# Adding two recurrences' sums by accumulating DMAs instead of on VectorE, in an attention and feed-forward kernel

## The chip, the cores and the metric

The kernel runs on one NeuronCore of a Trainium2 chip. The metric is the device time of one execution in microseconds (us); lower is better.

## The reference, cut to what matters

Four sequences (B = 4) of 256 tokens with 256 channels pass through one layer: a gate, causal attention with 16 heads, a second gate, and a feed-forward part with ternary weights.

```python
def _bi_wkv(r, k, v, w, u, time_emb):            # both gates; k and v are the same side input
    tf = sigmoid(sum(time_emb, axis=-1))[:, None, None]
    decay = exp(-exp(w))[None, :] * (0.5 + 0.5 * tf[:, :, 0])
    ek = exp(minimum(k, 30.0)); ekv = ek * v
    # nf, df: a = a * decay + ekv_t, b = b * decay + ek_t over the tokens; nb, db: the same in reverse
    euk = exp(minimum(u[None, None, :] + k, 30.0))
    num = nf + nb - ekv + euk * v
    den = df + db - ek + euk
    return sigmoid(r) * (num / maximum(den, 1e-08)) * (0.8 + 0.2 * tf)
x = x + attention(_bi_wkv(x, side, side, w1, u1, cond))
h = _bi_wkv(x, side, side, w2, u2, cond)
x = x + (silu(h @ ternary(W_up).T) * (h @ ternary(W_gate).T)) @ ternary(W_down).T
```

## The kernel before, in words

Channels lie on the 128 partitions, in two tiles (`ct`) of 256 tokens, so one sequence of one quantity is 128x512 in f32. Everything is in SBUF after the first loads. Each engine has its own program, written out by hand, and the engines are ordered by semaphores alone.

**A gate.** For gate `c` (0 the first, 1 the second) and sequence `b`, `ek[b % 3]` holds the products (half 0) and the exponentials (half 1). Four forward scans (`forward`, L599, two per half, 128x256 each) write `fwd[c]`, and four backward scans (`backward`, L611) write `bwd[c]`. `extra[c]` holds exp(u + k), made on ScalarE, and its product with k, made on GpSimd (`extra_products`, L245). `add_extra` adds `extra[c]` into `fwd[c]` and `sums` adds `bwd[c]` into it, each one instruction of 128x1024. `bound_denominator` (L628) bounds the denominator, ScalarE takes its reciprocal as a logarithm and an exponential (`first_reciprocal`, L358 and L360), `refine` does two products on VectorE, and `first_wkv` or `second_wkv` gives the gate's output. For sequences 0 and 1 the first gate is done in one piece by `first_gate`.

**Attention.** The gate's output goes through the projections of keys and queries (L980) and of values (L990). ScalarE and VectorE split keys and queries into f16 halves (`high_halves`, `low_halves`), six DMAs of SP stack them (`stack<-halves`), and PE makes scores in six groups (`scores`). VectorE takes row maxima (`maxima`), PE turns them, SP stores them in the stack, PE makes transposed scores (`score_t`), ScalarE exponentiates (`exp_probs`), and PE weighs the values (`weigh`). After the last `weigh` come the row reciprocals on ScalarE (L406, L408), `normalize` on VectorE (L690), `project` on PE (L1207) and `residual` on VectorE (L696).

**Feed-forward.** With f = b - 1, iteration `b` does the feed-forward part of sequence f beside the attention scores of sequence b. `ffn_input` multiplies 1 + tanh with the second gate's output (L705) into `x2`; ScalarE rounds it to `x2_hi` in f16 (`high_input`, L437), and `low_input` (L710) gives `x2_lo`. `up_gate(f, e)` for the eight tiles `e` of hidden channels (L1015) takes both halves; ScalarE does the silu (L445), VectorE the product (`gate`, L753). Two tiles are a group `g`: ScalarE rounds it (`high_hidden`, L452), GpSimd subtracts (`low_hidden`, L270), and `down(f, g)` (L1043) multiplies by the down weights; the last group is split on VectorE (`last_halves`). `finish` writes the result.

**Order.** VectorE alternates `maxima(b, j)` and `gate(f, j)` for j from 0 to 5, then does gates 6 and 7 with other work of the gates between them. In this text, turn b to b + 1 is the stretch from the last `weigh` of b to the third group of scores of b + 1. The last sequence has a tail in two halves of tokens.

Of the kernel before, what the change touches and what calls it, by code (L numbers as in the profile page):

```python
# [44 lines left out]
def build(nc, x_d, k_d, cond_d, vec_d, wqkv_d, wo_d, wup_d, wgate_d, wdown_d, out_d):  # L45
    with ExitStack() as ctx:
# [78 lines left out]
        w_in = [sem(f"w_in{i}") for i in range(3)]  # L125
        k_top_done, roundneg_made = sem("k_top_done"), sem("roundneg_made")
# [108 lines left out]
        def _(pool):  # L235
# [12 lines left out]
            def add_extra(c, b):  # L248
# [38 lines left out]
            values_of_keys(0)  # L287
            extra_products(0, 0)
# [16 lines left out]
            extra_products(0, 1)  # L305
            bound_keys()
            pool.wait_ge(vec_in, 16)
            bound_sums(1)
            bound_sums(0)
            values_of_keys(2)  # L310
            for b in range(1, B):
                more = b + 1 < B
                if more:
                    if b == 1:
                        pool.wait_ge(x2lo_done, b)
                    pool.wait_ge(fwd_done[0], 4 * b + 8)
# [8 lines left out]
                low_hidden(b - 1, 1)  # L325
                low_hidden(b - 1, 2)

        @block.scalar
        def _(act):
# [13 lines left out]
            def extra_exp(c, b):  # L343
                if b:
                    act.wait_ge(fwd_extra[c], b)
# [145 lines left out]
            def ternary_weights(i):  # L491
# [3 lines left out]
                nc.scalar.activation(w_tern[i][:, :], w_raw[i][:, :], ACT.Sign,  # L495
                                     bias=round_neg[:, 0:1]).then_inc(tern_done, 1)

            for b in range(B):
                more, f = b + 1 < B, b - 1
                if b:  # L500
# [6 lines left out]
                    high_input(f)  # L507
# [4 lines left out]
                    if b == 1:  # L512
                        ternary_weights(2)
# [861 lines left out]
```

## Time and profile before

| | |
|---|---|
| time, median of 3 runs | 180.51 us (178.92 to 180.75) |
| the profiled execution's own time | 180.7 us |
| its span, first to last instruction | 178.9 us |
| outside the span | 1.8 us |
| mean granted TensorE clock | 0.985 of full |
| busy: PE, VectorE (DVE), ScalarE (ACT), GpSimd (POOL) | 147.7, 154.7, 116.5, 53.2 us |

The rows further down come from that one execution. In a timeline a row is: start us, duration us, engine, line, operation, tiles, shapes, count, and in brackets how long the engine had been idle before it and what ended that. Matmuls overlap in the pipeline, so their rows' durations overlap too, and the distance from start to start is the better measure.

### The profile page before, as it was taken

The page shows a single profiled execution, that of the slowest core. Times are in us where ns is not written, and L with a number is a line of the kernel's source. Part 1 is how long each engine was busy: PE and PEld are TensorE (multiplying, and loading weights), DVE is VectorE, ACT ScalarE, POOL GpSimd, SP SyncE. Part 2 cuts the span into 40 slices and gives each one's busy share as a digit, 9 for nine tenths or more (in the row PEclk, how much of TensorE's full clock was granted, in tenths as well). Part 3 has the DMA queues.
Part 4 walks back from the last instruction along what each step waited for, and adds up shares of the span by engine and source line. Part 5 has one row for each costly group of instructions (what it writes and reads, how often), then busy time and mean ns, then how long its engine had stood idle before and what let it go on. Part 6 is the DMA issues. An engine that isn't in the chain of part 4 may idle for free. (4 is left out here: it accounts for less than half of the span.)

```text
span 178.9 us, 3837 instructions
## 1 busy us (share of the span) xinstructions
PE 147.7 (83%) x1550; PEld 98.8 (55%) x1550; DVE 154.7 (86%) x259; ACT 116.5 (65%) x187; POOL 53.2 (30%) x51
## 2 busy tenths in 40 slices
PE   0007897968949998999998899999989999997991
PEld 0007882233337854774676457745855576686870
DVE  0599998999998778999999999999697999986672
ACT  2547986989645795479557734885574458875640
POOL 8920052999600049440000194400002223000000
PEclk9999999999996999999999999999999999999997
DMA  4999322000000310000033000000420000010001
GB/s 107 359 430 421 121 75 103 4 2 0 5 0 0 119 60 0 0 5 0 0 132 108 0 4 0 2 4 0 148 92 0 2 5 0 4 62 2 4 0 59
DMA packets 5706, 10.91 MB, mean 61 GB/s; under 512 B 760, under 2 KB 4024, under 8 KB 5304
## 3 DMA queue, kind: packets, MB, share of 16 engines
q1 hardware_dynamic: 5400, 10.52, 15.5%
q8 instruction: 12, 0.20, 0.5%
q10 hardware_dynamic: 288, 0.14, 0.4%
q14 instruction: 6, 0.05, 0.1%
HBM read 6.43 MB, written 1.05 MB: 42 GB/s over the span
## 5 line engine op out<-in xcount | busy, mean ns | idle before, releaser
L245 POOL TENSOR_TENSOR extra<-extra,k_t 128x512 f32<-128x512 f32 x8 | 10.3, 1293 | 79.3 <-DVE fwd L599 40.2
L686 DVE TENSOR_REDUCE row_max<-wide 128x4 f32<-128x1024 f32 (+1 forms) x24 | 28.8, 1217 | 1.0 <-PE wide L1070 1.0
L401 ACT ACTIVATE probs<-wide 128x1024 f32<-128x1024 f32 x24 | 23.8, 1018 | 1.1 <-PE wide L1095 0.7
L445 ACT ACTIVATE silu<-attn_ps,up_scale 128x256 f32<-128x256 f32 x24 | 11.2, 472 | 19.5 <-PE attn_ps L1015 17.6
L611 DVE TENSOR_TENSOR_SCAN bwd<-ek,decay 128x255 f32<-128x255 f32 x32 | 21.2, 707 | 0.0
L599 DVE TENSOR_TENSOR_SCAN fwd<-decay,ek 128x256 f32<-128x256 f32 x32 | 21.1, 706 | 0.0
L1215 PE MATMUL wide<-ones 128*128 128x128 f32 x24 | 5.4, 425 | 14.5 <-DVE fwd L804 14.5
L270 POOL TENSOR_TENSOR hid_lo<-hid,hid_hi 128x512 f16<-128x512 f32 x9 | 12.4, 1379 | 15.1 <-ACT hid_hi L452 15.1
L1117 PE MATMUL attn_ps<-probs,v_pad 128*32 128x256 f32 (+1 forms) x192 | 12.6, 334 | 3.6 <-ACT probs L401 3.6
L1015 PE MATMUL attn_ps<-x_hi,w_tern 128*128 128x256 f16 x96 | 14.2, 274 | 1.3 <-ACT x_hi L437 0.8
L1015 PE MATMUL attn_ps<-x_lo,w_tern 128*128 128x256 f16 x96 | 13.9, 273 | 0.0
L1065 PE MATMUL wide<-mask_qk,identity_b 128*128 128x256 bf16 (+1 forms) x48 | 11.0, 311 | 2.9 <-DMA stack<-halves 1.8
L1215 PEld LDWEIGHTS wide<-ones 128*128 128x128 f32 x24 | 5.2, 331 | 14.5 <-issue 14.5
L1117 PE MATMUL attn_ps<-probs,ones_pad 128*32 128x256 f32 (+1 forms) x192 | 12.4, 331 | 0.0
L753 DVE TENSOR_TENSOR hid<-silu,attn_ps 128x256 f32<-128x256 f32 x24 | 9.9, 411 | 2.8 <-ACT silu L445 2.7
L1015 PEld LDWEIGHTS attn_ps<-x_hi,w_tern 128*128 128x128 f16 x96 | 8.3, 98 | 5.1 <-issue 2.2
L263 POOL TENSOR_SCALAR uk_top<-k_t,vec 128x768 f32<-128x768 f32 (+1 forms) x4 | 11.0, 2738 | 0.4
L1043 PE MATMUL acc_ps<-hid_hi,w_tern 128*128 128x256 f16 x64 | 9.8, 273 | 0.5 <-DVE hid_hi L769 0.5
L1015 PEld LDWEIGHTS attn_ps<-x_lo,w_tern 128*128 128x128 f16 x96 | 9.2, 98 | 1.3 <-DVE x_lo L710 0.2
L358 ACT ACTIVATE rec<-fwd 128x512 f32<-128x512 f32 x8 | 5.0, 631 | 7.4 <-DVE fwd L628 4.0
L980 PE MATMUL turn_ps<-wkv,wqkv 128*128 128x256 f32 x32 | 9.4, 445 | 0.5 <-DVE wkv L657 0.5
L1043 PE MATMUL acc_ps<-hid_lo,w_tern 128*128 128x256 f16 x64 | 9.7, 273 | 0.0
(147 smaller groups left out, 346.4 us busy)
## 6 DMA issues: line engine op xcount, KB each, us to landing
stack<-halves SPq DMA_DIRECT2D x24, 128.0 KB, 2.1
w_raw<-wup_d SPq DMA_DIRECT2D x1, 1024.0 KB, 11.3
w_raw<-wgate_d SPq DMA_DIRECT2D x1, 1024.0 KB, 13.0
w_raw<-wdown_d SPq DMA_DIRECT2D x1, 1024.0 KB, 14.9
out_d<-x_t SPq DMA_DIRECT2D x4, 256.0 KB, 2.3
wqkv<-wqkv_d SPq DMA_DIRECT2D x1, 768.0 KB, 7.0
k_t<-k_d SPq DMA_DIRECT2D x1, 768.0 KB, 8.4
x_t<-x_d SPq DMA_DIRECT2D x1, 768.0 KB, 9.8
```

What stands on the lines that cost most here:

```text
L263: nc.gpsimd.tensor_scalar(uk_top[c][:, :, ct * T:(ct + 1) * T], k_t[:, 2 - c:B, ct, :], vec[:, u:u + 1], CLAMP, ALU.add, ALU.min).then_inc ...
L270: nc.gpsimd.tensor_tensor(hid_lo[:, g % 2], hid[:, g % 2], hid_hi[:, g % 2], ALU.subtract).then_inc(hidlo_done, 1)
L401: nc.scalar.activation(probs[:, j, :], flat(wide[j % 2][:, :, :]), ACT.Exp, scale=SOFTMAX_SCALE).then_inc(prob_done, 1)
L445: nc.scalar.activation(silu[:, e % 2], up, ACT.Silu, scale=up_scale[:, 0:1]).then_inc(silu_done, 1)
L599: nc.vector.tensor_tensor_scan(fwd[c][:, half, ct * T:(ct + 1) * T], d, ek[b % 3][:, half, ct * T:(ct + 1) * T], 0.0, ALU.mult, ALU.add).t ...
L611: nc.vector.tensor_tensor_scan(bwd[c][:, half, at], ek[b % 3][:, half, after], d, 0.0, ALU.add, ALU.mult).then_inc(bwd_done[c], 1)
L686: nc.vector.tensor_reduce(out, src, AX.X, ALU.max).then_inc(max_done, 1)
L1015: mm = nc.tensor.matmul(attn_ps[:, e % 2, w * T:(w + 1) * T], w_tern[w][:, at:at + P], half[:, dt, :], start=(w == 0 and dt == 0 and x == ...
L1043: mm = nc.tensor.matmul(acc_ps[:, dt, :], w_tern[2][:, at:at + P], half[:, g % 2, e, :], start=first, stop=(g == NG - 1 and e == EG - 1 an ...
L1065: nc.tensor.matmul(tile[:, a, :, width - P:width], identity_b[:, :], mask_qk[:, :].unsqueeze(1).broadcast_to([P, per, P]), start=True, sto ...
L1117: mm = nc.tensor.matmul(attn_ps[lo:lo + 32, what, ct * T + q0:(ct + 1) * T], left, prob[:, i % 2, i // 2, :], start=(j == 0), stop=(second ...
L1215: nc.tensor.matmul(wide[0][:, 0, 0:P], ones[:, :], ones[:, :], start=True, stop=True)
```

## The change

- **Sums by DMA.** `send_extra` and `send_backward` are DMAs issued by GpSimd that add one tile of 128x1024 f32 (512 KB) into `fwd[c]` in SBUF. They take the place of `add_extra` and `sums` for the first gate of sequences 2 and 3 and the second gate of sequences 0, 1 and 2, ten DMAs in all. On VectorE eight instructions of 128x1024 go, on GpSimd two. The second gate of sequence 3 stays on VectorE. A pair of DMAs is a chain: the second waits until the first has landed, and GpSimd waits with it.
- **Scans moved.** The second gate's forward scans stand between gates 5, 6 and 7, where the first gate's last backward scans and `sums(0, b + 1)` stood (sequence 3: the second gate's backward scans). The first gate's scans of the next sequence follow `finish`, the low halves and `second_wkv`. For sequence 3 the second gate's backward scans stand at the turn.
- **Reciprocals.** `refine(1, b)` stands at the end of iteration b, ahead of `normalize`.
- **Feed-forward input.** `x2_hi` is written by VectorE (two instructions of 128x256), then `x2` by one of 128x512; `high_input` on ScalarE is gone. No scans stand any more between `ffn_input` and `maxima(b, 0)`.
- **Group 2.** `down(f, 2)` does both halves ahead of the first transposed scores, where its low half followed two groups of them.
- **Start and weights.** The first two products of sequence 0 go from GpSimd to VectorE. The down weights' last step on ScalarE is done in two pieces, after silu 1 and silu 3, where it stood whole ahead of silu 0. `bound_sums(0)` comes ahead of `bound_sums(1)` on GpSimd.

```diff
+            def send_extra(c, b):
                 pool.wait_ge(prod_done[c], b + 1)
                 pool.wait_ge(fwd_done[c], 4 * b + 4)
-                nc.gpsimd.tensor_tensor(fwd[c][:, :, :], fwd[c][:, :, :], extra[c][:, :, :],
-                                        ALU.add).then_inc(fwd_extra[c], 1)
+                pool.dma_start(fwd[c][:, :, :], extra[c][:, :, :], accum_op=ALU.add).then_inc(extra_in[c], 16)
+
+            def send_backward(c, b):
+                wait_extra_added(pool, c, b)
+                pool.wait_ge(bwd_done[c], 4 * b + 4)
+                pool.dma_start(fwd[c][:, :, :], bwd[c][:, :, :], accum_op=ALU.add).then_inc(sum_in[c], 16)
...
-            values_of_keys(0)
-            extra_products(0, 0)
...
             def extra_exp(c, b):
                 if b:
-                    act.wait_ge(fwd_extra[c], b)
+                    wait_extra_added(act, c, b - 1)
...
                     for e in range(ET):
                         silu_up(f, e)
                         if e % EG == 0 and e:
                             high_hidden(f, e // EG - 1)
+                        if b == 1 and e in (1, 3):
+
+                            ternary_weights(2, slice(1024 * (e // 2), 1024 * (e // 2 + 1)))
...
                     dve.wait_ge(tanh1_done, 2 * b + ct + 1)
-                    nc.vector.scalar_tensor_tensor(x2[:, part], x2[:, part], 1.0, wkv2[:, b, part],
-                                                   ALU.add, ALU.mult).then_inc(x2_done, 1)
-
-            def low_input(b):
+                    nc.vector.scalar_tensor_tensor(x2_hi[:, ct, :], x2[:, part], 1.0, wkv2[:, b, part],
+                                                   ALU.add, ALU.mult).then_inc(x2hi_done, 1)
                 dve.wait_ge(x2hi_done, 2 * b + 2)
+                nc.vector.scalar_tensor_tensor(x2[:, :], x2[:, :], 1.0, wkv2[:, b, :],
+                                               ALU.add, ALU.mult).then_inc(x2_done, 1)
+                dve.wait_ge(x2_done, b + 1)
...
                     up_gate(f, 7)
-                    down(f, 2, 0)
+                    down(f, 2)
```

VectorE in iteration 2, from gate 5 to the last group's halves, before:

```order
L753 TENSOR_TENSOR hid<-silu,attn_ps 128x256
L611 SCALAR_TENSOR_TENSOR bwd0<-ek0,decay 128x255 x2
L753 TENSOR_TENSOR hid<-silu,attn_ps 128x256
L623 TENSOR_TENSOR fwd0<-fwd0,bwd0 128x1024
L753 TENSOR_TENSOR hid<-silu,attn_ps 128x256
L760 CAST hid_hi<-hid 128x512
```

And after:

```order
L771 TENSOR_TENSOR hid<-silu,attn_ps 128x256
L616 SCALAR_TENSOR_TENSOR fwd1<-decay,ek2 128x256 x2
L771 TENSOR_TENSOR hid<-silu,attn_ps 128x256
L616 SCALAR_TENSOR_TENSOR fwd1<-decay,ek2 128x256 x2
L771 TENSOR_TENSOR hid<-silu,attn_ps 128x256
L778 CAST hid_hi<-hid 128x512
```

Four forward scans of the second gate stand there now in place of two backward scans and a sum of the first.

VectorE at the turn from sequence 2 to 3, from `first_wkv` on, before:

```order
L657 SCALAR_TENSOR_TENSOR wkv1<-fwd0,gain,err0 128x512
L599 SCALAR_TENSOR_TENSOR fwd1<-decay,ek2 128x256 x4
L784 SCALAR_TENSOR_TENSOR x_t<-acc_ps,out_scale,x_t 128x512
L617 TENSOR_TENSOR fwd1<-fwd1,extra1 128x1024
L623 TENSOR_TENSOR fwd1<-fwd1,bwd1 128x1024
L628 TENSOR_SCALAR fwd1<-fwd1 128x512
L671 SCALAR_TENSOR_TENSOR halves<-turn_ps,vec,halves 128x256 x2
L671 SCALAR_TENSOR_TENSOR halves<-acc_ps,vec,halves 128x256 x2
L690 TENSOR_TENSOR heads_t<-attn_ps,row_rec 128x512
L638 TENSOR_TENSOR err1<-fwd1,rec1 128x512
```

And after:

```order
L674 SCALAR_TENSOR_TENSOR wkv1<-fwd0,gain,err0 128x512
L802 SCALAR_TENSOR_TENSOR x_t<-acc_ps,out_scale,x_t 128x512
L645 TENSOR_SCALAR fwd1<-fwd1 128x512
L688 SCALAR_TENSOR_TENSOR halves<-turn_ps,vec,halves 128x256 x2
L628 SCALAR_TENSOR_TENSOR bwd1<-ek0,decay 128x255 x2
L688 SCALAR_TENSOR_TENSOR halves<-acc_ps,vec,halves 128x256 x2
L655 TENSOR_TENSOR err1<-fwd1,rec1 128x512
L660 SCALAR_TENSOR_TENSOR err1<-err1,rec1 128x512
L707 TENSOR_TENSOR heads_t<-attn_ps,row_rec 128x512
L679 SCALAR_TENSOR_TENSOR wkv2<-fwd1,gain,err1 128x512
L628 SCALAR_TENSOR_TENSOR bwd1<-ek0,decay 128x255 x2
```

The denominator (L628 before, L645 after) now stands behind `finish` and waits for the second DMA of its pair; two backward scans of sequence 3 stand ahead of the low halves of the queries. At the turn from 1 to 2 the first gate's four forward scans stand behind `finish` as well.

GpSimd in iteration 1, with the semaphores it waits for, after (before, the first DMA was an addition on GpSimd and the three others were not there):

```order
L263 TENSOR_TENSOR extra0<-extra0,k_t 128x512 [waits ex_exp0,x2lo_done]
L269 DMA fwd0<-extra0 128x1024 [waits fwd_done0,prod_done0]
L263 TENSOR_TENSOR extra1<-extra1,k_t 128x512 [waits ex_exp1]
L292 TENSOR_TENSOR hid_lo<-hid,hid_hi 128x512 [waits hidhi_done]
L257 TENSOR_TENSOR ek0<-ek0,k_t 128x512 [waits ek_exp]
L292 TENSOR_TENSOR hid_lo<-hid,hid_hi 128x512 [waits hidhi_done]
L274 DMA fwd0<-bwd0 128x1024 [waits bwd_done0,extra_in0]
L292 TENSOR_TENSOR hid_lo<-hid,hid_hi 128x512 [waits down_done,hidhi_done]
L269 DMA fwd1<-extra1 128x1024 [waits fwd_done1,prod_done1]
L274 DMA fwd1<-bwd1 128x1024 [waits bwd_done1,extra_in1]
```

The pair of the second gate follows the last `low_hidden`, and the next instruction of GpSimd waits for the next iteration.

## Rows read from the trace of the kernel before

**Rows 1.** Windows: us, busy time and count by engine, granted clock, DMA share

```profile
51.00:53.20 2.20, 0.01 (x2) 0.01 (x2) 2.13 (x4) 1.54 (x2) 0.00 (x0) 1.00 0.00 0
54.40:57.60 3.20, 3.20 (x12) 2.64 (x9) 3.00 (x6) 1.34 (x3) 0.00 (x0) 0.54 0.00 0
79.00:93.60 14.60, 14.60 (x196) 8.65 (x194) 14.32 (x24) 10.79 (x16) 0.43 (x1) 1.00 0.11 37
93.60:103.30 9.70, 7.98 (x57) 4.92 (x54) 9.34 (x18) 7.47 (x15) 1.13 (x1) 1.00 0.16 55
```

**Rows 2.** Timeline of PE, iterations 0 to 3

```profile
54.39 3.44 PE L980 MATMUL turn_ps<-wkv,wqkv 128*128 128x256 f32 x8
...
77.90 0.60 PE L1043 MATMUL acc_ps<-hid_hi,w_tern 128*128 128x256 f16 x4
...
91.74 0.42 PE L1117 MATMUL attn_ps<-probs,v_pad 128*32 128x128 f32 x8
...
93.62 1.99 PE L990 MATMUL wide<-wqkv,wkv 128*128 128x256 f32 x8
...
104.79 0.38 PE L1065 MATMUL wide<-mask_qk,identity_b 128*128 128x256 bf16 x2
...
129.17 1.99 PE L990 MATMUL wide<-wqkv,wkv 128*128 128x256 f32 x8
...
139.41 0.39 PE L1065 MATMUL wide<-mask_qk,identity_b 128*128 128x256 bf16 x2
```

**Rows 3.** Timeline of ACT: three places where it waits or sets the turn

```profile
51.59 0.63 ACT L348 ACTIVATE extra<-uk_top 128x512 f32<-128x512 f32 x1 [2.57 <-DVE fwd L617]
...
94.39 0.63 ACT L408 ACTIVATE row_rec<-row_rec 128x512 f32<-128x512 f32 x1
...
127.33 0.63 ACT L358 ACTIVATE rec<-fwd 128x512 f32<-128x512 f32 x1 [1.83 <-DVE fwd L628]
```

**Rows 4.** Groups of VectorE by line

```profile
L623 DVE TENSOR_TENSOR fwd<-fwd,bwd 128x1024 f32<-128x1024 f32 x6 | 7.3, 1222 | 0.1
...
L617 DVE TENSOR_TENSOR fwd<-fwd,extra 128x1024 f32<-128x1024 f32 x4 | 4.9, 1217 | 0.1
...
L628 DVE TENSOR_SCALAR fwd<-fwd 128x512 f32<-128x512 f32 x6 | 2.5, 424 | 0.1
```

**Rows 5.** Timeline of VectorE

```profile
6.55 1.27 DVE L584 TENSOR_SCALAR extra<-extra 128x512 f32<-128x512 f32 x1 [0.35 <-ACT extra L352]
...
8.42 0.77 DVE L816 TENSOR_SCALAR exp_t<-exp_t 128x4 f32<-128x4 f32 x1 [0.27 <-ACT exp_t L465]
...
50.35 1.21 DVE L617 TENSOR_TENSOR fwd<-fwd,extra 128x1024 f32<-128x1024 f32 x1
...
67.59 0.42 DVE L753 TENSOR_TENSOR hid<-silu,attn_ps 128x256 f32<-128x256 f32 x1 [1.03 <-ACT silu L445]
...
98.50 0.87 DVE L696 SCALAR_TENSOR_TENSOR x_t<-attn_ps,bo_v,x_t 128x256 f32<-128x256 f32 x2
99.54 0.76 DVE L705 SCALAR_TENSOR_TENSOR x<-x,wkv 128x256 f32<-128x256 f32 x2 [0.17 <-ACT x L431]
...
121.37 2.43 DVE L599 TENSOR_TENSOR_SCAN fwd<-decay,ek 128x256 f32<-128x256 f32 x4
...
147.41 2.18 DVE L611 TENSOR_TENSOR_SCAN bwd<-ek,decay 128x255 f32<-128x255 f32 x2
```

**Rows 6.** Timeline of GpSimd

```profile
6.28 1.26 POOL L239 TENSOR_TENSOR ek<-ek,k_t 128x512 f32<-128x512 f32 x1
...
77.42 2.01 POOL L270 TENSOR_TENSOR hid_lo<-hid,hid_hi 128x512 f16<-128x512 f32 x1 [2.73 <-ACT hid_hi L452]
...
147.63 1.41 POOL L270 TENSOR_TENSOR hid_lo<-hid,hid_hi 128x512 f16<-128x512 f32 x1 [2.73 <-ACT hid_hi L452]
```

**Rows 7.** DMA issues: KB each, us from issue to landing

```profile
stack<-halves SPq DMA_DIRECT2D x24, 128.0 KB, 2.1
w_raw<-wup_d SPq DMA_DIRECT2D x1, 1024.0 KB, 11.3
```

More of the change, by code:

```diff
@@ L125, in build @@
         w_in = [sem(f"w_in{i}") for i in range(3)]
+        extra_in, sum_in = ([sem(f"{n}{c}") for c in range(2)] for n in ("extra_in", "sum_in"))
         k_top_done, roundneg_made = sem("k_top_done"), sem("roundneg_made")
@@ L325, in _ @@
                 low_hidden(b - 1, 1)
+                if more:
+                    send_backward(0, b + 1)
                 low_hidden(b - 1, 2)
+                if more:
+                    send_extra(1, b)
+                    send_backward(1, b)
         @block.scalar
@@ L811, in _ @@
             clamp_keys(0)
+            dve.wait_ge(ek_done, 1)
+            nc.vector.tensor_tensor(ek[0][:, 0, :], ek[0][:, 1, :], flat(k_t[:, 0]), ALU.mult).then_inc(ekv_done, 1)
             clamp_extra(0, 0)
@@ L814, in _ @@
             nc.vector.tensor_reduce(tsum[:, :], cond_b[:, :, :], AX.X, ALU.add).then_inc(tsum_done, 1)
+            dve.wait_ge(ex_done[0], 1)
+            nc.vector.tensor_tensor(extra[0][:, 0, :], extra[0][:, 1, :], flat(k_t[:, 0]),
+                                    ALU.mult).then_inc(prod_done[0], 1)
             dve.wait_ge(expt_done, 1)
@@ L853, in _ @@
                         normalize(f)
+                        second_wkv(f)
                         if more:
-                            backward(0, b + 1, 1, (1,))
-                        refine(1, f)
-                        second_wkv(f)
+                            backward(0, b + 1, 0)
+                        else:
+                            backward(1, b, 0)
                     residual(f)
                     ffn_input(f)
-                    if more:
-                        forward(0, b + 1, 0, (0,))
-                    low_input(f)
-                    if more:
-                        forward(0, b + 1, 0, (1,))
                     maxima(b, 0)
@@ L937, in _ @@
                     dve.wait_ge(bo_done, 1)
-                    forward(0, 2, 1)
-                    backward(0, 2, 1)
+                    for half in (1, 0):
+                        forward(0, 2, half)
+                    for half in (1, 0):
+                        backward(0, 2, half)
                     first_product(1, 0)
@@ L1020, in up_gate, with down @@
                     mm.then_inc(ug_done, 1)
-            def down(b, g, halves=2):
+            def down(b, g):
                 parts = ((hid_hi, hidhi_done), (hid_lo, hidlo_done))
@@ L1029, in down @@
                         pe.wait_ge(y_done, b)
-                if b == 0 and g == 0:
-                    pe.wait_ge(tern_done, 3)
-                for half, done in parts if halves == 2 else parts[halves:halves + 1]:
+                if b == 0 and g % 2 == 0:
+                    pe.wait_ge(tern_done, 3 + g // 2)
+                for half, done in parts:
                     if g == NG - 1:
@@ L1046, in down @@
                                                   skip_group_check=True)
-                if halves:
-                    mm.then_inc(down_done, 1)
+                mm.then_inc(down_done, 1)
             def rows(b, side, a, pair, n, lo, hi):
@@ L1288, in _ @@
                     tail_score_t(1)
-                    down(f, 2, 1)
                     down(f, 3)
@@ L1300, in _ @@
                 score_t(b, 1)
-                down(f, 2, 1)
                 down(f, 3)
```

98 lines of the change are left out of this document (45 added, 53 removed).

## The prediction

> **What bounds the kernel now.** I read the windows first. Between 79.0 and 93.6 PE is busy for 14.60 of 14.60 us, and VectorE for 14.32 [rows 1]. Both are full, but PE alone has no idle time at all, so work that leaves VectorE there doesn't shorten the stretch. In the next window, the turn from sequence 1 to 2 (93.6 to 103.3), PE is busy 7.98 of 9.70 us. Next I read PE's timeline for where it is held. In iteration 0 it idles from 51.0 to 53.2 and then runs 3.2 us at a granted clock of 0.54, which is the lower of its two levels, 1.2 GHz [rows 1]; the key projection at 54.39 has a row of 3.44 us there, where eight matmuls of the same shape have 1.99 at 93.62 [rows 2]. Last I read what ScalarE waits for: 2.57 us on VectorE's addition L617 ahead of 51.59, and 1.83 us on L628 ahead of 127.33 [rows 3]. So the sums on VectorE cost time in two kinds of places: in iteration 0 and at the turns. In between, PE's own work decides.
>
> I take the change in five terms: start, iteration 0, group 2's low half, turns, tail. They are differences against the span of 178.9 us.
>
> **Start: -0.5.** The two products leave GpSimd. VectorE pays two instructions of about 0.67 us for it (1222 ns for 1024 columns is 0.61 for 512, plus start-up [rows 4]). But its own small steps there are drawn out today: the bounding at 6.55 takes 1.27 us beside GpSimd's product at 6.28, and exp_t, four columns, 0.77 [rows 5, 6]. The same kind of bounding takes 0.42 elsewhere (L628 [rows 4]), and four columns about 0.15. So VectorE wins 0.85 + 0.62 and fills idle time of 0.35 + 0.27 [rows 5] against 1.34 paid: 0.7 at best. ScalarE's step between tsum and exp_t keeps some of it. I take 0.5; the bounds are 0 and 0.7. All of iteration 0 hangs on this chain, so it moves everything.
>
> **Iteration 0: -2.7.** ScalarE's `extra_exp(1, 1)` now waits for a DMA issued some 15 us earlier, so the wait of 2.57 goes, the last exponential comes 3 us earlier, and PE starts the key projection when `wkv1` is there, near 51.0 where it was 54.39 [rows 2, 3]. That isn't the gain yet, since VectorE comes late next. Its list from 50.35 to gate 0 at 67.59 takes 17.24 us [rows 5]. The new list: the bounding 0.35; eight scans at 2.43 for four [rows 5], 4.85, where there were L617, L623 (2.44, [rows 4]) and four scans, so no gain yet; three products 1.8; low keys, `wkv2`, low queries 2.4; residual and the wait for tanh 1.1. That is 10.5, at 60.85. Then `x2_hi` 0.7, at 61.55, when PE can begin. PE's way from there: first halves 0.9, two groups of scores 1.75, low half of tile 0 0.45, silu 0.5 on ScalarE, so gate 0 at 65.15 at the latest; VectorE comes by 64.7 with its own list (x2 0.6, x2_lo 0.65, a maximum 1.15). The row of 67.59 shows 1.03 us of waiting for silu, behind the down weights' last step on ScalarE, which now stands behind silu 1. Gate 0 at 64.7 to 65.15 is 2.4 to 2.9 earlier. A new risk lies in it: PE is done with the query projection near 54.7 and waits for `normalize` until about 56.7, 2.0 us, nearly the 2.2 us after which its clock fell to 0.54 before [rows 1]. If it falls again, `project`, eight such matmuls, takes 1.5 more and the residual comes 0.5 later. I take -2.7 of -2.2 to -2.9.
>
> **Group 2's low half: +1.5.** `down(f, 2)` low now stands ahead of the transposed scores, in PE's full stretch. PE is done with the high half at 78.33 (77.90 and 0.44 for four matmuls [rows 2]). GpSimd's `hid_lo` starts at 77.42 and took 2.01 beside VectorE's sum, and 1.41 beside scans in iteration 3, where VectorE's two scans took 2.18 in place of 1.26 [rows 5, 6]. Now scans stand beside it in each iteration. With 1.41 it is there at 78.83, so PE idles 0.5, three times: +1.5. The bounds are 0.3 (1.16, uncontended) and 1.1 (2.01) each, so +0.8 to +3.3. VectorE's gate 7 comes 0.8 later for the drawn-out scans. That is hidden: PE does two groups of transposed scores (1.3 us) ahead of `down(f, 3)`, and the first gate's output, 0.55 later, still meets PE's key projection, which is 0.5 later itself.
>
> **Turns: -1.65.** I count on PE from `values` to the fourth group of scores: 93.62 to 104.79 is 11.17, 129.17 to 139.41 is 10.24 [rows 2]. The new chain from `values`: row reciprocals 1.3 (L406 and the row at 94.39 [rows 3]), `normalize` 0.65, project 1.85, so the residual starts at +3.95 where it was +4.88 (98.50 [rows 5]). From the residual to x2's first instruction 1.04 (98.50 to 99.54 [rows 5]), where `x2_hi` stands now, 0.7; x2 0.6; x2_lo 0.67. The low half is there at +7.0, PE's scores and high half are done by then, and low half 0.9 and the wait for a maximum (1.15 after x2_lo) bring the third group of scores to +8.35 and the fourth to +9.88, by the step of 1.53 between groups. That is 1.3 less at the turn 1 to 2 and 0.36 less at 2 to 3. The stack DMA has its source earlier too: the reciprocal ahead of the high queries no longer waits 1.83 [rows 3]. What carries this is VectorE's room: L617 and L623 (2.44) leave each turn and L623 the gates, 3.66 an iteration [rows 4], against some 0.7 for `x2_hi`. The first gate's scans that filled it (0.6 each) now lie in the shadow of `project` and of the query projection.
>
> **Tail: -0.2.** Sequence 3's denominator comes 2.4 us earlier (four scans [rows 5]), but ScalarE takes it only behind its fifth exponential, nearly as before, and PE's weighing behind it keeps its length. I take -0.2, bounds 0 and -0.5.
>
> **What the DMAs may cost: 0.** Nothing in the trace adds by DMA or is issued by GpSimd, so I bound one DMA (issue to landing, D). `stack<-halves` moves 128 KB in 2.1 us [rows 7]. The accumulation reads two tiles of 512 KB. The low end is that row, 2.1. In the loading phase 1024 KB landed in 11.3 us behind other loads, a slow row [rows 7]; that is 5.6 for 512 KB, and with 2 us for GpSimd's preparation, as long as it was at most over 512 columns (2.01 [rows 6]), the high end is 7.6. Neither row is near, the one small and the other crowded, so I take the middle, 4.8; the queues are nearly empty at these places (DMA share 0.11 to 0.16 [rows 1]). How much is free? The second gate's forward scans end at about 79.35 in the frame of the old trace. The denominator may be as late as 90.7: the query projection ends at 91.74 [rows 2], shifted by 0.5, the high halves take 0.8, and ahead of the low queries stand 0.35 + 0.8 + 1.2 of VectorE's work. 11.35 us for two DMAs: free up to D = 5.65, then 2 us for each us of D, at two turns, so 4(D - 5.65). For the first gate one DMA issued at about 74.7 must land by 80.9, D up to 6.2.
>
> The Trainium skill (DMA: Bandwidth & Descriptors, Anatomy of one DMA, SWDGE path) gives about 2.0 us + bytes / 436e3 for such a DMA, 3.2 us here without the addition; by that the DMAs stay hidden with over 2 us to spare, which no row here shows. The Trainium skill (SBUF — State Buffer, Who interferes with whom) states a rule against this change: descriptor generation on GpSimd is starved while VectorE is in a two-port mode, as its boundings of 0.42 us would be; that would add at most 0.4 to a D, and the sum stays as it is unless D is above 5.2 already.
>
> **Sum.** -0.5 - 2.7 + 1.5 - 1.65 - 0.2 = -3.55. The profiled execution took 180.7, so 177.15; the median of the runs is 0.2 lower, 180.51, so I say **177.0**. With the inner bounds of the terms the sum lies between -2.0 and -5.0, so 175.5 to 178.5.
>
> **Rivals.**
> - **The DMAs are slow (ends slower than before).** The mechanism: VectorE waits in `bound_denominator(1, b)` for the pair, with both low halves, the backward scans and `normalize` behind it, and scores wait for the stack. The place: both turns. The gain is used up at 4(D - 5.65) = 3.55, D = 6.5. At D = 7.5 it costs 7.4: 184.4. Between 5.9 and 7.1 the result is within 1%. For it: two reads and a write, unknown unit. Against: empty queues. 0.12 for within 1%, 0.14 for slower by more.
> - **GpSimd's low half is late.** It takes 2.0 as at 77.42 [rows 6], PE loses 1.1 three times: +3.3 in place of 1.5, and the clock falls once more in iteration 0: 179.1, within 1%. For it: that duration is what two of three iterations show today. Against: it stood beside `tensor_tensor`, which scans replace. 0.12.
> - **More than forecast.** `hid_lo` uncontended, the full start and iteration 0, tail -0.5: below 175.8. 0.10.
>
> **How the numbers follow.** The forecast has 0.52. A measurement of this kernel can tell about 1% from no change, so faster is below 178.7 and slower above 182.3. Faster: 0.52 + 0.10 = 0.62; same 0.12 + 0.12 = 0.24; slower 0.14. For 8 in 10 the range leaves out 0.07 below, and the upper part of the slow DMAs: 175.4 to 181.8.
>
> **What would show it.** (1) First scan near 9.7 where it was 10.2. (2) ScalarE without the wait at 51.6, the key projection at full clock near 50.5. (3) Gate 0 of iteration 1 at 64.2 to 64.7, the start included. (4) PE idle 0.3 to 1.1 ahead of `down(f, 2)` low. (5) D below 5.65, and no wait of VectorE in L645 that passes on to the low queries. (6) No wait of PE for the stack at the turns. The forecast is wrong if L645 waits over 2 us at a turn, or if PE's idle time between 79 and 93 grows by more than 1 us.

## The result, and the profile after

The kernel after takes **177.89 us** (median of 6 runs, 177.87 to 177.95), the kernel before 180.47 beside it (6 runs, 178.92 to 181.73): ratio 0.990, 95% interval 0.9858 to 0.9942. All ratios here leave out runs over 1.5% above a kernel's fastest. The profiled execution took 177.95, its span is 176.2 where it was 178.9. The forecast was 177.0, within 175.4 to 181.8: the direction came true, the gain is 2.6 us where 3.5 was said.

One thing has to be known first. The kernel before has no single time. Its 74 runs beside all kernels of this study lie in three bands: 38 at 178.30 to 179.02 (median 178.86), 31 at 179.94 to 180.77 (median 180.49), 5 at 181.3 to 181.9. The profiled execution, 180.7, belongs to the second. The six runs of the kernel after lie in one band, 0.08 us wide. Against the first band it gains 1.0 us, against the second 2.6.

The timeline of PE of the kernel after, at the rows that answer to [rows 2]:

```profile
37.71 2.29 PE L1009 MATMUL attn_ps<-mask_kq,identity_b 128*128 128x512 bf16 x5
...
51.43 1.99 PE L992 MATMUL turn_ps<-wkv,wqkv 128*128 128x256 f32 x8
...
55.84 1.99 PE L1218 MATMUL attn_ps<-heads_t,wo 128*128 128x256 f32 x8 [0.70 <-DVE heads_t L707]
...
75.44 0.61 PE L1055 MATMUL acc_ps<-hid_lo,w_tern 128*128 128x256 f16 x4 [0.39 <-POOL hid_lo L292]
75.89 0.38 PE L1101 MATMUL wide<-mask_kq,identity_b 128*128 128x256 bf16 x2
...
90.71 1.99 PE L1002 MATMUL wide<-wqkv,wkv 128*128 128x256 f32 x8
...
98.24 1.05 PE L1027 MATMUL attn_ps<-x_lo,w_tern 128*128 128x256 f16 x8 [0.62 <-DVE x_lo L728]
99.37 0.39 PE L1076 MATMUL wide<-mask_qk,identity_b 128*128 128x256 bf16 x2
...
101.00 0.39 PE L1076 MATMUL wide<-mask_qk,identity_b 128*128 128x256 bf16 x2
...
125.96 1.99 PE L1002 MATMUL wide<-wqkv,wkv 128*128 128x256 f32 x8
```

The key projection has 1.99 us at full clock instead of 3.44. Group 2's low half waits 0.39 us for GpSimd (0.40 at 110.69 and 0.39 at 145.93). `values` of sequence 2 comes at 90.71 where it was 93.62, and the fourth group of scores at 101.00 where it was 104.79. The windows of the kernel after over the places of [rows 1] (us, busy time and count of PE, PEld, DVE, ACT, POOL, granted clock, DMA share, GB/s):

```profile
51.00:53.20 2.20, 2.20 (x28) 1.82 (x19) 2.20 (x5) 1.77 (x3) 0.00 (x0) 1.00 0.00 0
...
76.00:90.70 14.70, 14.70 (x197) 8.57 (x194) 12.95 (x25) 10.78 (x16) 1.73 (x2) 1.00 0.50 118
90.70:101.00 10.30, 9.40 (x70) 5.88 (x67) 9.57 (x16) 6.57 (x12) 2.44 (x3) 1.00 0.12 41
```

PE has no idle time left from 51.0 to 53.2, stays full in the stretch of the transposed scores, and in the turn idles 0.90 us instead of 1.72. (The last window runs on to the fourth group of scores; before, it is 1.72 us to that point too, in the window 93.6 to 104.8.) ScalarE's timeline where [rows 3] has the wait of 2.57 us:

```profile
48.39 0.62 ACT L371 ACTIVATE extra<-uk_top 128x512 f32<-128x512 f32 x1
49.34 1.03 ACT L424 ACTIVATE probs<-wide 128x1024 f32<-128x1024 f32 x1 [0.32 <-PE wide L1106]
```

It is gone. VectorE's timeline at the start, at gate 0 and at the turn, its bounding at the second turn, then GpSimd's, then the DMA issues (KB each, us to landing), which answer to [rows 5 to 7]:

```profile
6.99 0.51 DVE L601 TENSOR_SCALAR extra<-extra 128x512 f32<-128x512 f32 x1
...
9.36 1.27 DVE L616 TENSOR_TENSOR_SCAN fwd<-decay,ek 128x256 f32<-128x256 f32 x2
...
64.14 0.42 DVE L771 TENSOR_TENSOR hid<-silu,attn_ps 128x256 f32<-128x256 f32 x1 [0.62 <-ACT silu L462]
...
86.61 0.43 DVE L645 TENSOR_SCALAR fwd<-fwd 128x512 f32<-128x512 f32 x1 [0.73 <-DMA fwd<-bwd]
86.96 0.87 DVE L688 SCALAR_TENSOR_TENSOR halves<-turn_ps,vec,halves 128x256 f16<-128x256 f32 x2
87.74 1.26 DVE L628 TENSOR_TENSOR_SCAN bwd<-ek,decay 128x255 f32<-128x255 f32 x2
89.81 0.88 DVE L688 SCALAR_TENSOR_TENSOR halves<-acc_ps,vec,halves 128x256 f16<-128x256 f32 x2 [0.81 <-ACT halves L404]
```

```profile
121.42 0.43 DVE L645 TENSOR_SCALAR fwd<-fwd 128x512 f32<-128x512 f32 x1 [2.64 <-DMA fwd<-bwd]
```

```profile
73.99 1.40 POOL L292 TENSOR_TENSOR hid_lo<-hid,hid_hi 128x512 f16<-128x512 f32 x1 [1.93 <-ACT hid_hi L469]
76.49 0.87 POOL L269 DMA_DIRECT2D fwd<-extra  x1 [1.10 <-DVE fwd L616]
82.16 0.85 POOL L274 DMA_DIRECT2D fwd<-bwd  x1 [4.80 <-ACT extra L371]
```

```profile
fwd<-extra POOLq DMA_DIRECT2D x5, 512.0 KB, 5.2
fwd<-bwd POOLq DMA_DIRECT2D x5, 512.0 KB, 4.5
```

The pair is issued at 76.49 and 82.16. VectorE waits 0.73 us for it in L645, but then again 0.81 us for ScalarE's high queries ahead of the low ones, so nothing of the first wait is passed on. At the second turn it waits 2.64 us in L645, since the four scans of 2.43 us that stand ahead of it at the first turn aren't there, and then 1.25 us for the high queries. These wait 0.71 us for TensorE in their turn, so that wait isn't passed on either.

### The profile page after: what moved, and what is told of

It is laid out like the page before. It is cut to its first block, busy times and chain, and to the rows that moved or that the text cites. A ratio compares the mean times of both kernels' runs of the same rounds, so it can differ in the third digit from the quotient of the medians.

```text
span 176.2 us, 3834 instructions
## 1 busy us (share of the span) xinstructions
PE 147.7 (84%) x1550; PEld 97.2 (55%) x1550; DVE 148.5 (84%) x256; ACT 115.1 (65%) x182; POOL 54.4 (31%) x57
## 4 chain that ended last, share of the span: by engine, by line
PE 37%; DVE 22%; issue 6%; ACT 4%; POOL 2%; POOLq 1%; DVEq 0%; ACTq 0%
PE attn_ps L1128 7%; DVE row_max L703 7%; PE acc_ps L1055 4%; PE attn_ps L1027 4%; PE wide L1206 3%; PE wide L1101 2%; DVE hid L771 2%; PE attn_ps L1218 2%; PE wide L1106 2%; PE acc_ps L992 2%; PE turn_ps L992 2%; POOL hid_lo L292 2%; PE attn_ps L1170 2%; DVE bwd L628 1%; PE turn_ps L1183 1%
## 5 line engine op out<-in xcount | busy, mean ns | idle before, releaser
L263 POOL TENSOR_TENSOR extra<-extra,k_t 128x512 f32<-128x512 f32 x7 | 9.7, 1382 | 62.6 <-DVE x_lo L728 43.8
L616 DVE TENSOR_TENSOR_SCAN fwd<-decay,ek 128x256 f32<-128x256 f32 x32 | 23.1, 770 | 0.0
L628 DVE TENSOR_TENSOR_SCAN bwd<-ek,decay 128x255 f32<-128x255 f32 x32 | 20.0, 677 | 0.0
L1226 PE MATMUL wide<-ones 128*128 128x128 f32 x24 | 4.5, 369 | 13.7 <-DVE fwd L822 13.7
L292 POOL TENSOR_TENSOR hid_lo<-hid,hid_hi 128x512 f16<-128x512 f32 x9 | 11.1, 1238 | 15.4 <-ACT hid_hi L469 15.4
L1226 PEld LDWEIGHTS wide<-ones 128*128 128x128 f32 x24 | 4.3, 282 | 13.7 <-issue 13.7
L285 POOL TENSOR_SCALAR uk_top<-k_t,vec 128x512 f32<-128x512 f32 (+1 forms) x4 | 11.1, 2769 | 0.4
L1081 PE MATMUL wide<-stack 63*128 63x128 f16 (+1 forms) x128 | 9.4, 246 | 0.0
L1101 PE MATMUL wide<-mask_kq,identity_b 128*128 128x256 bf16 (+1 forms) x36 | 8.5, 319 | 0.0
```

Of the source, the lines that this page charges most:

```text
L285: nc.gpsimd.tensor_scalar(uk_top[c][:, :, ct * T:(ct + 1) * T], k_t[:, 2 - c:B, ct, :], vec[:, u:u + 1], CLAMP, ALU.add, ALU.min).then_inc ...
L292: nc.gpsimd.tensor_tensor(hid_lo[:, g % 2], hid[:, g % 2], hid_hi[:, g % 2], ALU.subtract).then_inc(hidlo_done, 1)
L616: nc.vector.tensor_tensor_scan(fwd[c][:, half, ct * T:(ct + 1) * T], d, ek[b % 3][:, half, ct * T:(ct + 1) * T], 0.0, ALU.mult, ALU.add).t ...
L628: nc.vector.tensor_tensor_scan(bwd[c][:, half, at], ek[b % 3][:, half, after], d, 0.0, ALU.add, ALU.mult).then_inc(bwd_done[c], 1)
L1101: nc.tensor.matmul(tile[:, a, :, 0:P], identity_b[:, :], mask_kq[:, :].unsqueeze(1).broadcast_to([P, per, P]), start=True, stop=False, ski ...
```

## Experiments

### The bands of the kernel before: is it the clock?

In the profiled execution of before, TensorE waits 2.60 us for the last `probs` of iteration 0, and then runs at 0.54 of its clock [rows 1, 2]:

```profile
53.19 0.43 PE L1117 MATMUL attn_ps<-probs,v_pad 128*32 128x128 f32 x8 [2.60 <-ACT probs L401]
```

The experiment fills that wait:

```diff
                             weigh(0, j - 1)
+                    pe.wait_ge(neg_done, 1)
+                    keep_busy(8, flat(turn_ps[:, :, :]))
                     weigh(0, NT - 1)
```

> Changed: the kernel before, with eight filler matmuls (bf16, 512 columns, into a bank that is overwritten later) ahead of the last weighing of iteration 0, where TensorE waits 2.60 us for ScalarE's last exponential. Nothing is left out. The runs of the kernel before lie at 178.3 to 179.0 us (16 of 34 in the last two comparisons), near 180.5 (most of the others) and at 181.3 to 181.9; its profiled run shows the clock at 0.54 for some 3 us behind that wait. Theory: the levels are whether the clock falls there, and the fall costs 1.6 us. With TensorE busy through the wait the clock stays, and all runs lie at 178.9, within 0.3 us. Then 1.6 of the 2.6 us that the change gained are the clock's, and only 1.0 the work's. Rival: the levels have another cause (transfers, the start), and the spread from 178.3 to 181.9 stays.

Measured: 178.88 us, 12 runs: 9 at 178.45 to 179.03, 3 at 179.52 to 179.56, further off than the 0.3 us expected; nothing near 180.5 or above, where 12 of the 23 runs of before beside it lie (180.17 to 181.85). The ratio to before is 0.9977 (0.9946 to 1.0008). PE's timeline of this run and its windows:

```profile
51.04 1.90 PE L997 MATMUL turn_ps<-mask_kq,identity_b 128*128 128x512 bf16 x8
53.22 0.43 PE L1117 MATMUL attn_ps<-probs,v_pad 128*32 128x128 f32 x8 [0.28 <-ACT probs L401]
...
54.23 1.99 PE L980 MATMUL turn_ps<-wkv,wqkv 128*128 128x256 f32 x8
```

```profile
54.23:57.60 3.37, 3.37 (x20) 2.98 (x17) 3.37 (x7) 2.37 (x5) 0.00 (x0) 1.00 0.00 0
```

The last weighing starts at the same time as before (53.22, it was 53.19), so the work waits as long; only the clock is kept. Gate 0 then stands at 65.98 instead of 67.59 [rows 5]: **1.61 us** of the profiled execution are the clock's. This is the distance between the two lower bands. Why three runs took 179.5 isn't shown: none of them was profiled. Their mean granted clock is the lowest of the twelve, 0.980 and 0.981 beside 0.984 to 1.000, which speaks for a smaller fall elsewhere.

Two limits. First, no run of before in its lowest band was profiled. That the clock stays at this place in those runs follows from this experiment alone. Their mean granted clock doesn't tell: 0.977 to 0.990 in the lowest band, 0.981 to 0.990 in the second (only the highest band stands out, with 0.968). Second, a fall can cost nothing. In the profiled executions of this kernel and of the kernel after, the granted clock is 0.57 on average over 4 us (38 to 42 and 37 to 41), which it isn't in that of before. In after, five matmuls at 37.71 take 2.29 us there, in before 1.24. Yet this kernel's last weighing comes at 53.22 as said, and of the kernel after one run with a mean clock of 0.981 and one with 1.000 took 177.89 and 177.88. What counts is where the clock falls.

### The start alone

The kernel before, with `values_of_keys(0)` and `extra_products(0, 0)` off GpSimd and on VectorE:

```diff
-            values_of_keys(0)
-            extra_products(0, 0)
...
+            nc.vector.tensor_tensor(ek[0][:, 0, :], ek[0][:, 1, :], flat(k_t[:, 0]), ALU.mult).then_inc(ekv_done, 1)
...
+            nc.vector.tensor_tensor(extra[0][:, 0, :], extra[0][:, 1, :], flat(k_t[:, 0]),
+                                    ALU.mult).then_inc(prod_done[0], 1)
```

> Changed: the kernel before, with the start of the kernel after alone: the two extra products of sequence 0's first gate on VectorE. Nothing is left out. Theory: the start is a term of its own, worth the 0.84 us by which the first scan moved in the kernel after: 180.47 - 0.8 = 179.7 us. Rival: in the kernel before iteration 0 waits for something else (values, a later load), which takes some of it back: 180.2 or more.

Measured: bands again, 7 of 12 runs at 177.88 to 177.90, 4 at 179.50 to 179.55, one at 180.84; ratio to before 0.9929 (0.9886 to 0.9972). The lowest band is 0.97 under that of before, and **as low as the whole change** (177.89). The forecast of 179.7 was worked out from a median that mixes bands; band by band its 0.8 comes near. The profiled run is one of the second band; its windows show where the clock went, behind the same wait of 2.60 us:

```profile
50.00:52.30 2.30, 0.08 (x4) 0.08 (x8) 2.23 (x4) 1.54 (x2) 0.00 (x0) 1.00 0.00 0
52.30:53.90 1.60, 1.60 (x32) 1.26 (x32) 1.60 (x4) 1.26 (x2) 0.00 (x0) 0.54 0.00 0
53.90:57.00 3.10, 3.10 (x14) 2.56 (x11) 2.63 (x5) 1.33 (x3) 0.00 (x0) 0.69 0.00 0
```

So in the lowest band the start is worth all of the change's 1.0 us, and everything else in it comes out at about nothing.

### Group 2's low half back where it was

```diff
-                    down(f, 2)
+                    down(f, 2, 0)
...
                 score_t(b, 1)
+                down(f, 2, 1)
                 down(f, 3)
```

> Changed: the kernel after, with the low half of group 2 put back behind the first two groups of transposed scores, where the kernel before has it. Nothing is left out. Theory: the low half's new place costs 0.54 to 0.58 us in each of three iterations (PE waits 0.39 to 0.40 us for GpSimd's low half, and VectorE's scans beside it are drawn out). Moved back, the low half is awaited by nobody: 177.89 - 1.5 to 1.7 = 176.2 to 176.4 us. Rival: the 0.4 us are only taken from another wait, of the transposed scores for VectorE's or ScalarE's work behind it, and the time stays at 177.9. A second rival: the low half comes later for group 3, whose hidden tiles take the same buffer, and PE waits there: over 178.2.

Measured: 178.09 us (178.05 to 178.11), 0.992 of before (0.9888 to 0.9952): 0.2 **slower** than after. The first rival came true, and the trace names the wait that takes over, in iterations 1 and 2 (iteration 2 has the same row at 111.39, with 0.74):

```profile
71.20 0.88 POOL L274 DMA_DIRECT2D fwd<-bwd  x1
72.44 0.55 SPq L243 DMA_DIRECT2D stack<-neg_max  x1
75.80 0.39 PE L1102 MATMUL wide<-mask_kq,identity_b 128*128 128x256 bf16 x2 [0.73 <-DMA stack<-neg_max]
```

This is the transfer of the maxima, 8 KB, issued by SP at 72.44; the transposed scores need it. In the kernel before it was issued at 75.88, the scores began at 78.33, 2.45 us later, and TensorE didn't wait. In this run it takes 3.36 us from the issue to the scores. In iteration 3 the scores start without a wait and this kernel gains about 0.57 on after. The difference between the iterations: in 1 and 2 GpSimd has just issued `fwd<-bwd` of the first gate (71.20), 512 KB; in iteration 3 there is no such DMA.

Two kernels test that. The first has the low half behind in iteration 3 alone (`down(f, 2, 2 if more else 0)`), the second keeps it behind everywhere and takes the first gate's DMAs away instead:

```diff
-            return b >= 2 if c == 0 else b < B - 1
+            return c == 1 and b < B - 1
...
-                    send_extra(0, b + 1)
+                    add_extra(0, b + 1)
...
+                    sums(0, b + 1)
                     bound_denominator(0, b + 1)
```

> Changed: the kernel after, with group 2's low half behind the first two groups of transposed scores in iteration 3 alone; in iterations 1 and 2 it stands as in the kernel after. Nothing is left out. Theory: the earlier place pays where an accumulating DMA of the first gate is in the way of the small transfer of the maxima (TensorE waited 0.73 and 0.74 us for it in iterations 1 and 2 when the low half stood behind, and not at all in iteration 3, which has no such DMA). So iteration 3 alone gains what the low half costs there, 0.57 us: 177.3 to 177.4. Rival: the wait for the maxima isn't tied to the DMA, and iteration 3 gains nothing: 177.9.

> Changed: the kernel after with group 2's low half behind the first two groups of transposed scores in all iterations, and with the first gate's two sums of sequences 2 and 3 as instructions (the addition on GpSimd, the sum on VectorE ahead of its bounding); the second gate keeps its DMAs. Nothing is left out. Theory: with no accumulating DMA under way when the maxima are sent, TensorE's waits of 0.73 and 0.74 us for their transfer go. VectorE's 1.22 us come back ahead of the key projection, where some 0.35 us are free, so 0.9 is lost: 178.09 - 1.47 + 1.7 = 178.3, between 177.5 and 178.6. Rival: the maxima's transfer is late for a cause of its own (its queue, its start 0.2 us nearer to the scores) and the waits stay: 179.5 or more.

Measured: 177.36 us (177.35 to 177.48; ratio 0.989, 0.9845 to 0.9934), as the theory said; and 179.33 (179.31 to 179.53; 0.9987, 0.9956 to 1.0017). The second is 1.0 slower than forecast and near its rival's time, yet its rows decide between the two. The window 72.4 to 76.0 (columns as in the windows above), first with the low half back and the DMA in the air, then without the DMA, and the issue of the maxima and the scores of the latter:

```profile
72.40:76.00 3.60, 2.87 (x27) 2.26 (x24) 3.60 (x6) 2.33 (x5) 1.40 (x1) 1.00 0.74 148
```

```profile
72.40:76.00 3.60, 3.60 (x34) 2.71 (x32) 3.60 (x6) 2.33 (x5) 1.41 (x1) 1.00 0.01 2
```

```profile
72.61 0.55 SPq L243 DMA_DIRECT2D stack<-neg_max  x1
...
75.06 0.38 PE L1107 MATMUL wide<-mask_kq,identity_b 128*128 128x256 bf16 x2
...
84.37 1.99 PE L997 MATMUL turn_ps<-wkv,wqkv 128*128 128x256 f32 x8 [0.94 <-DVE wkv L678]
```

With a DMA share of 0.01 the maxima, issued at 72.61, are there by 75.06, in 2.45 us or less, and PE doesn't wait. The cost is on the other side: VectorE's 1.22 us come back, and the key projection waits 0.94 for `wkv1`. Another 0.44 goes because TensorE, which comes 0.74 earlier, now meets VectorE's halves of group 3 unfinished (its matmuls at 76.94 and 77.67 don't follow at once). That is 1.38 lost for 0.74 gained, at each of two places, where 0.9 was expected. The Trainium skill (Trainium Kernel Development and Optimization, Key Constraints) says that DMAs from all issuing queues run on the same 16 engines and interleave; a small transfer of SP beside a large one of GpSimd is that, and the trace agrees: 3.36 against at most 2.45 us.

### How much room has the pair?

```diff
+                if c == 1 and b:
+                    pool.wait_ge(tern_done, 1)
+                    pool.dma_start(w_raw[0][:, 0:1024].rearrange("p (a q) -> p a q", a=2), extra[1][:, :, :]).then_inc(copy_in, 16)
+                    pool.wait_ge(copy_in, 16 * b)
                 pool.dma_start(fwd[c][:, :, :], extra[c][:, :, :], accum_op=ALU.add).then_inc(extra_in[c], 16)
```

> Changed: the kernel after, with one more DMA of 512 KB on GpSimd's queue (a plain copy of extra[1] into a tile that is free by then), awaited ahead of the accumulating pair of the second gate in iterations 1 and 2. Nothing is left out. Theory: the pair has little room, about 0.8 us at the first turn and 1.25 at the second (by those much the high queries on ScalarE end what the low queries on VectorE wait for). A copy that takes 4 us to land then passes on 3.2 + 2.75 us: about 183.8, between 182 and 185.5 for a copy of 3.2 to 4.8 us. Rival: the pair has room beyond what these waits show, since the rows behind it shift together: below 180.

Measured: 184.77 us (184.59 to 184.85), 1.030 of before (1.0252 to 1.0342). GpSimd's and VectorE's timelines at the first turn:

```profile
76.46 0.61 POOL L272 DMA_DIRECT2D w_raw<-extra  x1 [1.11 <-issue]
80.72 0.87 POOL L274 DMA_DIRECT2D fwd<-extra  x1 [3.65 <-DMA w_raw<-extra]
85.48 0.86 POOL L279 DMA_DIRECT2D fwd<-bwd  x1 [3.88 <-DMA fwd<-extra]
```

```profile
91.77 0.43 DVE L650 TENSOR_SCALAR fwd<-fwd 128x512 f32<-128x512 f32 x1 [5.92 <-DMA fwd<-bwd]
```

The bounding comes 5.16 later than in after (86.61); less the 0.81 of room that is 4.35. From `values(2)` to `values(3)` the kernel takes 40.66 us instead of 35.25, 5.41 more: the rest is `project`, which ran 3.13 us instead of 1.99, behind 4.46 us of waiting. At the second turn VectorE waits 2.71 more than in after, less 1.25 of room 1.46, and the remaining time is 1.3 longer. The room was read rightly. From the issue of one DMA to that of the next it took 4.26 and 3.22 us behind the two plain copies, and 4.76 and 4.71 behind the accumulating DMAs that follow them.

### Without the moved scans, and without the DMAs

Two kernels take the change apart. One is the kernel before with `send_sums(b)`, the pair in one piece on GpSimd, in place of `add_extra(1, b)` and `sums(1, b)` for `b` = 1, 2. The other is the kernel after with `by_dma` returning `False` and `add_extra` and `sums` of both gates back.

> Changed: the kernel before, with the second gate's addition and sum of sequences 1 and 2 as a pair of accumulating DMAs, and its scans, forward and backward, where the kernel before has them. Nothing is left out. Theory: the order is what hides the DMAs. The pair takes 5.2 + 4.5 us from the end of the scans near 88, so the bounding comes near 98 where it came at 91.3, and each turn is some 6 to 7 us longer: 192 to 195 us. Rival: the first DMA overlaps the low halves and the sum is short of that, with 3 to 4 us a turn: 187 to 189. If the DMAs could be hidden wherever they stand, it would be 179 or less.

Measured: 199.51 us (197.80 to 201.14), 1.106 of before (1.0969 to 1.1153). VectorE and PE at the first turn:

```profile
100.11 0.43 DVE L646 TENSOR_SCALAR fwd<-fwd 128x512 f32<-128x512 f32 x1 [11.61 <-DMA fwd<-bwd]
```

```profile
104.73 3.78 PE L1226 MATMUL attn_ps<-heads_t,wo 128*128 128x256 f32 x8 [9.52 <-DVE heads_t L708]
```

The first DMA went out at 88.46 and the second at 95.67, so 7.2 us for the first beside 4.4 for the second, and all of it in the open (at the second turn 5.6 for the first). Why the one took 7.2 isn't shown. PE's wait of 9.52 costs the clock besides: `project` has 3.78 for 1.99. The forecast of 6 to 7 a turn had neither.

> Changed: the kernel after in its order, with the sums of both gates as instructions again: the second gate's two on VectorE ahead of its bounding, the first gate's addition on GpSimd and its sum on VectorE. Nothing is left out. Theory: the DMAs carry the gain. In iteration 0 ScalarE waits for VectorE's addition again and VectorE has 2.4 us more (+2.4); at the two turns and in the gates 2.4 and 1.2 us of VectorE's work come back, of which some 0.8 to 1 us lie on the path each time: 182 to 183 us, slower than the kernel before by about 1%. Rival: the order of scans and products carries it, and the DMAs hardly matter: 178 to 179.

Measured: 183.81 us (183.74 to 183.87), 1.0245 of before (1.020 to 1.029), above the 182 to 183 expected. `values(1)` comes 2.88 later than in after: the wait for `probs` is back (2.85 us) and the clock falls behind it.

```profile
54.23 3.04 PE L991 MATMUL turn_ps<-wkv,wqkv 128*128 128x256 f32 x8
```

From `values(1)` to `values(2)` it takes 0.86 more than in after, from there to `values(3)` 2.03. So the new order without the DMAs is 3.3 to 5 us worse than the kernel before (by its two lower bands), and the old order with the second gate's DMAs 19 to 21: order and DMAs belong together.

### The ternary step, and the high half

The first has `ternary_weights(2)` whole ahead of silu 0. The second gives the rounding of x2 back to ScalarE:

```diff
-                    nc.vector.scalar_tensor_tensor(x2_hi[:, ct, :], x2[:, part], 1.0, wkv2[:, b, part],
-                                                   ALU.add, ALU.mult).then_inc(x2hi_done, 1)
+                    nc.vector.scalar_tensor_tensor(x2[:, part], x2[:, part], 1.0, wkv2[:, b, part],
+                                                   ALU.add, ALU.mult).then_inc(x2_done, 1)
```

> Changed: the kernel after, with the ternary step of the down weights (1.99 us on ScalarE) whole ahead of the first silu of iteration 1, where the kernel after has it in two halves behind silu 1 and silu 3. Nothing is left out. Theory: ScalarE stands idle 2.05 us ahead of silu 0 (63.64), which covers the 1.99, so the new place earns nothing and the time stays within 0.3 us of 177.89; it may gain some 0.2. Rival: the split is a part of iteration 0's gain (forecast with 1.03 us of waiting for silu ahead of gate 0): then 178.4 to 178.9.

Measured: 177.94 us (177.94 to 177.95), no difference to after: the split isn't a part of the gain.

> Changed: the kernel after, with the high half of the feed-forward input on ScalarE as in the kernel before (VectorE writes x2 first, ScalarE rounds it). Nothing is left out. Theory: at the turns VectorE's x2_hi (0.71 us) stands ahead of x2 and x2_lo; without it the low half is ready some 0.5 us earlier, though PE's first high half comes 0.3 later, and the third group of scores with it: 0.15 to 0.3 us in each of three iterations, 177.0 to 177.4. Rival: PE's high half is what counts, since the wait for the low half was only 0.62 us: 178.2 to 178.8.

Measured: 177.64 us (177.63 to 177.73), 0.9877 of before (0.9828 to 0.9926), 0.25 under after, where 0.5 to 0.9 was expected. In PE's timeline at the turn the high half waits 0.39 for ScalarE, the low one no longer for VectorE:

```profile
90.97 1.99 PE L1006 MATMUL wide<-wqkv,wkv 128*128 128x256 f32 x8
...
97.15 1.17 PE L1031 MATMUL attn_ps<-x_hi,w_tern 128*128 128x256 f16 x8 [0.39 <-ACT x_hi L460]
98.22 1.05 PE L1031 MATMUL attn_ps<-x_lo,w_tern 128*128 128x256 f16 x8
```

`values` to the low half is 7.25 instead of 7.53. In iteration 1, where PE waits for the high half itself, 0.26 is lost (90.97 for 90.71).

### What adds up

> Changed: the kernel after, with both edits: group 2's low half behind the first two groups of transposed scores, and the high half of the feed-forward input on ScalarE. Nothing is left out. Theory: they act at different places (79 and 95 to 99 in the frame of the kernel before) and add up: 175.5 to 176.0. Rival: the second earns nothing, and the time is that of the first alone, 176.3.

Measured: 177.76 us (177.74 to 177.79), 0.9883 of before (0.9829 to 0.9938), 0.12 above the high half alone. Theory and rival both took the low half's old place for a gain, and it costs, as above. With the low half behind in iteration 3 alone:

> Changed: the kernel after with the two edits that each gained: group 2's low half behind the transposed scores in iteration 3 alone (177.36 by itself), and the high half of the feed-forward input on ScalarE (177.64 by itself). Nothing is left out. Theory: they act at different places, 147 and 95 to 99 us, and add: 177.89 - 0.53 - 0.25 = 177.1 us. Rival: iteration 3 comes earlier by the one, and meets the same wait in the tail; the time is that of the better alone, 177.35.

Measured: **177.05 us** (177.03 to 177.07), 0.9874 of before (0.9826 to 0.9922), the fastest here, as the sum of the two gains said. It is 0.84 under after; its last row of a low half in iteration 3 has no wait:

```profile
146.78 0.61 PE L1059 MATMUL acc_ps<-hid_lo,w_tern 128*128 128x256 f16 x4
```

## Why the prediction was right, and where it wasn't

**Start, -0.5: -0.84.** Right in mechanism, too small. The first scan starts 9.36 where it was 10.20. VectorE's bounding took 0.51 us, near the 0.42 of [rows 4], and exp_t came earlier as well, so almost nothing of the gain was kept by ScalarE. This term alone is the gain in the lowest band. Single executions scatter here: with this change alone the scan starts at 9.23, and in the kernel with the unmoved pair, whose start is that of before, at 9.74.

**Iteration 0, -2.7: -2.61, but of two kinds.** Gate 0 moved by 3.45, less the start. Against the kernel that is kept busy it moves by 1.84, so the work is 1.00 shorter, and 1.61 is the clock. What went wrong is the first reading, "and then runs 3.2 us at a granted clock of 0.54": it took one execution's clock for the kernel's, and "the median of the runs is 0.2 lower" for a sign of agreement. About half of the runs of before lie in the lowest band, which is where the kernel kept busy lies, so by that experiment they have no fall there. The three runs shown, 178.92, 180.51 and 180.75, already lie in two bands. The fear for `project` did not come true: PE waited 0.70 us there and the eight matmuls took 1.99. One sum is off: VectorE's own items after 61.55 (0.6, 0.65 and 1.15) end at 63.95, not 64.7. PE's path, 65.15, was the later of the two in any case; without the gain at the start gate 0 came at 64.98.

**Group 2's low half, +1.5: +1.69 as a difference, and not what it costs.** GpSimd took 1.40 (1.41 was said) and PE waited 0.39 (0.5 was said); by the shift of the rows behind it 0.54, 0.58 and 0.57 were lost. But moved back it loses 0.36 more in iteration 1 and in 2 (178.09 against 177.36). What went wrong is "What the DMAs may cost: 0": it asked what waits for the DMAs and not what shares the way with them. The first gate's DMA delays the maxima, which makes the new place the better one in these two iterations. How much of the two differences would go without that DMA isn't shown, since there VectorE's halves hold PE next.

**Turns, -1.65: -0.83**, the largest miss, with the mechanism right and the size off. From `values` to the fourth scores it takes 10.29 at both turns, 0.88 less at the first, 0.05 more at the second; 9.88 was forecast. The excess builds up along the chain: `project` starts at +2.18 and the residual 2.03 later, at +4.21 where +3.95 was said; x2_lo ends at +7.47 for +7.0; the third group of scores comes at +8.66 for +8.35, the fourth after a step of 1.63 for 1.53. Part of the forecast's marks have no item behind them: 1.3, 0.65 and 1.85 make +3.80, not +3.95, and +7.0 and 1.15 make +8.15, not +8.35. `x2_hi` on VectorE is a part: back on ScalarE the low half starts 0.28 earlier.

**Tail, -0.2: -0.11.** Within its bounds.

**DMAs.** D was 4.5 and 5.2 beside 4.8 forecast, under 5.65, and nothing was passed on. The 4.8 was the middle between two rows called far, 2.1 and 7.6, so that it came out this near is luck. The room is not: 11.35 us for the pair less the 10.12 from 76.49 to 86.61 leaves 1.23, 0.81 and 1.25 are in the rows, and the third DMA confirms it. One sign misled. The forecast was to be wrong if L645 waits over 2 us at a turn, and it waited 2.64 at the second. Still nothing was lost: the wait measures how early VectorE arrives, and since it idles another 1.25 us for the high queries behind it, an earlier landing would have gained nothing there. The rival of slow DMAs had its mechanism right, as the third DMA shows: 7.5 us of copies cost 6.9. Its bounds for within 1%, D of 5.9 to 7.1, are by its own formula 6.1 to 7.0. Whether VectorE's boundings hold up GpSimd's preparation of a DMA, no run here shows.

**The sum.** The terms measured give -2.7, as the spans do. With iteration 0's 1.61 of clock left out they give -1.1, and against the lowest band 1.0 was measured.

## What to carry to other kernels

Before costing a wait in one profiled execution, look at how the runs lie. Here the second band and a granted clock of 0.54 behind an idle stretch belong together, and closing that stretch gains 1.6 us in about half of the runs and nothing in the others. When work moves from an engine to a DMA, list the small transfers that are in flight with it; a move of independent work into their wait (here the low half) can be right in the iterations with the DMA and wrong in the one without.

## What the runs showed that was not expected

- An accumulating DMA of 512 KB from on-chip memory to on-chip memory, issued by GpSimd, took 4.4 to 5.2 us from issue to landing (medians of three or five), and once, in the kernel with the unmoved pair, 7.2 to the next issue. In the kernel with the third DMA the medians are 4.5 us for accumulating DMAs and 3.5 for the two plain copies of the same size. The Trainium skill (DMA: Bandwidth & Descriptors, Anatomy of one DMA, SWDGE path) gives 3.2 by its fit, an estimate without the addition: the plain copies are 0.3 above, the accumulating ones 1.2 to 2. GpSimd is occupied 0.85 to 1.06 us for an accumulating issue, 0.61 for a plain one.
- One and the same kernel fell into its upper bands in 36 of 74 runs. Filling 1.9 us of TensorE's wait of 2.6 us removed the band at 180.5 in 12 runs, and none of the 6 runs of the kernel after, without that wait, left its 0.08 us.
